# Layer 0 of a four-layer attention stack: queue order, PSUM buffers and row transfers of the attention loop

## The reference, cut to layer 0

```python
h = jnp.concatenate([x, latents], axis=1)
q = (latents @ q_w + q_b).reshape(b, k_len, NH, DH)
kv = (h @ kv_w + kv_b).reshape(b, p + k_len, NH, DH, 2)
kmat, v = (kv[..., 0], kv[..., 1])
attn = jnp.einsum('bkhd,bnhd->bhkn', q, kmat) / DH
attn = jnp.where(full_mask[:, None, None, :], attn, -jnp.inf)
attn = jax.nn.softmax(attn.astype(jnp.float32), axis=-1)
attn_out = jnp.einsum('bhkn,bnhd->bkhd', attn, v).reshape(b, k_len, H)
attn_out = attn_out @ out_w + out_b + residual
out = rmsnorm(attn_out, postnorm_w)
out = jax.nn.gelu(out @ mlp_w1 + mlp_b1) @ mlp_w2 + mlp_b2
return out + residual
```

## Time and profile before

| what | us |
|---|---|
| median of 3 runs | 867.13 (861.98 to 872.77) |
| the profiled execution's own time | 865.07 |
| its span | 863.3 |
| TensorE busy with matmuls | 732.3 (85%) |
| VectorE, ScalarE, GpSimd busy | 502.7, 319.0, 310.6 |
| mean granted TensorE clock | 0.893 |

### The profile page before, as it was taken

One profiled execution on the slowest core, in us unless ns is written; L12 is line 12 of the kernel. 1 busy time (PEld: TensorE's weight loads), 2 busy tenths in 40 slices (PEclk: granted clock), 3 DMA queues, 4 the chain that ended last, 5 costly groups with the idle time before them and its releaser, 6 DMA issues.

```text
span 863.3 us, 11707 instructions
## 1 busy us (share of the span) xinstructions
PE 732.3 (85%) x4432; PEld 526.8 (61%) x4432; DVE 502.7 (58%) x840; ACT 319.0 (37%) x693; POOL 310.6 (36%) x292
## 2 busy tenths in 40 slices
PE   7479885858579687886999999999998999786798
PEld 5356553434259554555776678787566888354587
DVE  6433454554354749986553867433579667388453
ACT  1033322323141137774554222565223241376321
POOL 2020334322202438885330755000467523177200
PEclk7657776787879899999999999999999999987799
DMA  5615444300100050000345000043000000200000
GB/s 171 181 44 152 145 133 119 101 3 1 30 2 1 1 194 1 2 1 2 99 147 179 17 1 0 12 155 128 1 1 0 1 1 1 98 1 0 1 19 32
DMA packets 42073, 46.99 MB, mean 54 GB/s; under 512 B 7009, under 2 KB 36514, under 8 KB 41890
## 3 DMA queue, kind: packets, MB, share of 16 engines
q1 hardware_dynamic: 41456, 45.62, 17.1%
q10 hardware_dynamic: 562, 0.62, 0.3%
HBM read 37.88 MB, written 8.29 MB: 53 GB/s over the span
## 4 chain that ended last, share of the span: by engine, by line
PE 60%; DVE 22%; POOL 5%; issue 4%; DMA 4%; ACT 3%; SPq 2%; ACTq 0%; POOLq 0%; DVEq 0%
PE narrow_ps L459 8%; PE wide_ps L790 7%; PE wide_ps L440 6%; PE narrow_ps L825 5%; PE narrow_ps L638 5%; PE wide_ps L576 4%; PE wide_ps L741 4%; DMA wstream<-in_wqT 3%; PE wide_ps L777 3%; PE wide_ps L490 3%; DVE mx L1407 3%; PE wide_ps L764 2%; DVE scoresb L1334 2%; DVE mx L1343 2%; POOL probs L1633 2%
## 5 line engine op out<-in xcount | busy, mean ns | idle before, releaser
L1624 POOL TENSOR_TENSOR scoresb<-scoresb,mx 128x768 f32<-128x768 f32 (+1 forms) x40 | 70.7, 1767 | 152.9 <-DVE mx L1341 115.1
L1407 DVE TENSOR_REDUCE mx<-wide_ps 128x2 f32<-128x640 f32 x64 | 52.7, 823 | 62.0 <-PE wide_ps L576 62.0
L1633 POOL TENSOR_TENSOR probs<-scoresb,rcp 128x1024 f32<-128x1024 f32 x40 | 77.2, 1929 | 8.0 <-DVE rcp L1351 8.0
L1012 ACT ACTIVATE probsT<-wide_ps 128x1024 f32<-128x1024 f32 x40 | 40.9, 1023 | 105.3 <-PE wide_ps L490 105.3
L459 PE MATMUL narrow_ps<-wstream_r,hidden 128*128 128x256 f32 x576 | 71.9, 285 | 8.0 <-DVE hidden L1319 7.7
L576 PE MATMUL wide_ps<-krow,qrow 49*128 49x64 f32 (+2 forms) x192 | 41.7, 451 | 42.5 <-DVE mx L1407 37.5
L459 PEld LDWEIGHTS narrow_ps<-wstream_r,hidden 128*128 128x128 f32 x576 | 70.9, 192 | 9.5 <-DVE hidden L1319 8.2
L1610 POOL TENSOR_TENSOR rstd<-veps,mhalf 128x1 f32<-128x1 f32 x56 | 32.0, 572 | 121.1 <-DVE veps L1264 121.1
L440 PE MATMUL wide_ps<-xq_r,wstream_r 128*128 128x512 f32 x192 | 64.0, 416 | 9.8 <-issue 5.2
L490 PEld LDWEIGHTS wide_ps<-ident,probs 128*128 128x128 f32 x320 | 39.5, 151 | 48.2 <-issue 47.5
L490 PE MATMUL wide_ps<-ident,probs 128*128 128x128 f32 x320 | 46.3, 292 | 26.5 <-POOL probs L1633 24.7
(11 more groups left out here) (181 smaller groups left out, 1625.7 us busy)
## 6 DMA issues: line engine op xcount, KB each, us to landing
wstream<-in_L_xattn_wk SPq DMA_DIRECT2D x8, 512.0 KB, 4.1
wstream<-in_L_xattn_wv SPq DMA_DIRECT2D x8, 512.0 KB, 5.2
wstream<-in_L_xattn_wo SPq DMA_DIRECT2D x8, 512.0 KB, 6.4
wstream<-in_wqT SPq DMA_DIRECT2D x8, 512.0 KB, 7.9
kscratch<-kparts SPq DMA_DIRECT2D x24, 160.0 KB
krow<-kscratch SPq DMA_DIRECT2D x16, 200.0 KB
qscratch<-qparts SPq DMA_DIRECT2D x24, 128.0 KB
qrow<-qscratch SPq DMA_DIRECT2D x16, 192.0 KB
```

The source lines that it names most:

```text
L1012: nc.scalar.activation(dst, src, ACT.Identity, **kw).then_inc(ring.drained[ring.slot(key)], 1)
L1407: v.tensor_reduce(mx0[:, half % 2, qh, pl:pl + 3:2], ps[:, :, 0:KEYS0], AX, ALU.max).then_inc(wide.drained[wide.slot(key)], 1)
L1624: g.tensor_tensor(s3[:, first:], s3[:, first:], mx[:, u % 3, first:].unsqueeze(2).broadcast_to([P, 16 - first, n_scores]), ALU.subtract).t ...
L1633: g.tensor_tensor(probs[:, u % 2, :].rearrange("p (h k) -> p h k", h=16), s3[:, :, 0:T], rcp[:, u % 3, :].unsqueeze(2).broadcast_to([P, 16 ...
```

## The change

- GpSimd: key sums are issued by `sums_after`: the first three of a group at its last step, the fourth at the next step, each behind that step's rstd. Row additions start at step 9.
- PSUM: maxima alternate between wide buffers 1 and 2; wide buffer 0 is all that is left to the `quarter` ring, two 1-bank buffers. Both of a step's units of maxima follow the scores, "C" follows the maxima (`scores_ctx0`), then the first side job, values, the other jobs. The values' chunks are dealt out as 3, 2, 3.
- Rows: `qscratch` and `kscratch` are laid out head by head. A group's q is stored by 2 DMAs instead of 3, k by 2 instead of 3, k loaded by 3 instead of 4. Context keys come first in `kparts`, the products for them are placed accordingly.
- Start: the constant rows are stored from SP's queue ahead of the values' weights, k of group 0 is stored and loaded from ScalarE's queue after job ("k", 1); SP's order of x, bias and ctxD is new; GpSimd sets slots 1 and 2 of `krow` and `qrow`; ("vctx", 1) moves behind the second half's maxima; the first four units are turned before the other four run.

```diff
-        quarter = Ring([sem(f"quarter{i}_filled") for i in range(4)], [sem(f"quarter{i}_drained") for i in range(4)])
-        quarter_ps = wide_ps[:, 0:2, :].rearrange("p s (h n) -> p (s h) n", h=2)
+        quarter = Ring([sem(f"quarter{i}_filled") for i in range(2)], [sem(f"quarter{i}_drained") for i in range(2)])
+        quarter_ps = wide_ps[:, 0, :].rearrange("p (h n) -> p h n", h=2)
...
-        START0 = [("q", 0), ("k", 0), ("q", 1), ("k", 1), ("v", 0), ("q", 2), ("k", 2), ("vctx", 0), ("vctx", 1)]
+        START0 = [("q", 0), ("k", 0), ("q", 1), ("k", 1), ("v", 0), ("q", 2), ("k", 2), ("vctx", 0)]
-        START_MAX0 = [(half, pl, qh) for half in range(2) for pl in range(2) for qh in range(2)]
-        VALUES0 = {1: (0, 3), 2: (3, 6), 3: (6, 8)}
+        START_MAX0 = [[(half, pl, qh) for pl in range(2) for qh in range(2)] for half in range(2)]
+        VALUES0 = {1: (0, 3), 2: (3, 5), 3: (5, 8)}
+        def sums_after(step):
+            g, p = divmod(step, PAIRS0)
+            if p == 3 and g < GROUPS0:
+                return [step - 3, step - 2, step - 1]
+            return [step - 1] if p == 0 and 0 < g <= GROUPS0 else []
+        def head_rows(scratch, g, first, count):
+            rows_ = scratch[g, :, 0:QK_ROWS].rearrange("h (d s) n -> h d s n", s=3)[:, :, first:first + count]
+            return rows_.rearrange("h d s n -> h d (s n)")
+        def store_q(queue, g):
+            queue.wait_ge(*narrow.empty(("q", g)))
+            queue.dma_start(head_rows(qscratch, g, 0, 1), part_rows(qparts, g, 1)).then_inc(qk_stored[g % 2], 16)
+            queue.dma_start(head_rows(qscratch, g, 1, 2), part_rows(qparts, g, 2)).then_inc(qk_stored[g % 2], 16)
...
+        def wait_slot(queue, g):
+            queue.wait_ge(rows_set[min(g % 3, 1)], 2)
+            if g == 0:
+                queue.wait_ge(const_stored, 80)
...
+            queue.wait_ge(qk_stored[g % 2], 64 * (g // 2 + 1))
+        def load_k(queue, g):
+            wait_slot(queue, g)
+            for i, to, lo, hi in ((0, 2 * T, T, KEYS0), (0, 0, 0, T), (1, T, 0, KEYS0)):
+                queue.dma_start(krow[64 * i:64 * i + QK_ROWS + 2, g % 3, :, to:to + hi - lo].bitcast(F32),
+                                kscratch[g, i::2, :, lo:hi].rearrange("r s n -> s r n")).then_inc(qk_loaded[g % 3], 16)
...
-                ps, filled = take_wide(("M", half, pl, qh), 1, (2,))
+                ps, filled = take_wide(("M", half, pl, qh), 1, (1, 2))
...
-            for unit in START_MAX0:
+            for unit in START_MAX0[0]:
                 max_scores0(*unit)
-            side_product0(("max", 0), (0, 1))
+            side_product0(("max", 0), SIDE)
+            for unit in START_MAX0[1]:
+                max_scores0(*unit)
+            side_product0(("vctx", 1), SIDE)
             for step in range(STEPS0 + 5):
                 g, p = divmod(step, PAIRS0)
                 if step < STEPS0:
                     scores0(step)
-                units = max_units(step)
-                if units:
-                    max_scores0(*units[0])
+                for unit in max_units(step):
+                    max_scores0(*unit)
+                if step < STEPS0:
+                    scores_ctx0(step)
...
             sp.dma_start(*halves(q_w0, t["L0_xattn_q_w"])).then_inc(load["q_w0"], 16)
             sp.dma_start(actT[:, :, 0:S], xT[:, :, 0:S]).then_inc(load["xT0"], 16)
+            v_load(0, "k_w0")
+            sp.wait_ge(maskrow_ready, 1)
+            for b in range(B):
+                sp.dma_start(kscratch[2 * b:2 * b + 2, :, QK_ROWS],
...
+            v_load(1, "v_w0")
...
+            store_q(sp, 0)
+            sp.dma_start(vbias0[:], t["v_b0"].rearrange("(a n) -> a n", a=1).broadcast_to([P, D])).then_inc(load["v_b0"], 16)
+            sp.dma_start(actT[:, :, S:2 * S], xT[:, :, S:2 * S]).then_inc(load["xT1"], 16)
+            store_q(sp, 1)
+            store_k(sp, 1)
+            load_q(sp, 0)
+            sp.dma_start(ctxD[:].rearrange("p c b a k -> p c (b a k)"), t["ctxD"].rearrange("(c p) n -> p c n", p=P)).then_inc(load["ctxD"], 16)
+            load_q(sp, 1)
+            load_k(sp, 1)
+            load_max(0)
...
             for job in START0:
                 side0_copy(job)
+                if job == ("k", 1):
+                    store_k(act, 0)
+                    load_k(act, 0)
...
-            v.memset(krow[:].rearrange("p a r n -> p (a r n)").bitcast(F32), 0.0).then_inc(rows_set, 1)
+            v.memset(krow[:, 0].rearrange("p r n -> p (r n)").bitcast(F32), 0.0).then_inc(rows_set[0], 1)
...
-                if step < STEPS0:
-                    sum_keys0(step)
                 for job, n in side0(step):
                     if job == "proj":
                         rstd_of(0, n)
+                for unit in sums_after(step):
+                    sum_keys0(unit)
```

More of the change, by code:

```diff
@@ L265, in build @@
         link_pool = sem("pool_step")
-        rows_set = sem("rows_set")
+        rows_set = [sem(f"rows_set{i}") for i in range(2)]
         maskrow_ready = sem("maskrow_ready")
@@ L546, in side_product0 @@
                     pe.wait_ge(load["ctxT"], 16)
-                    for off, size, src in ((0, S, actT[:, :, b * S:(b + 1) * S]), (S, T, ctxT[:, :, b * T:(b + 1) * T])):
+                    for off, size, src in ((T, S, actT[:, :, b * S:(b + 1) * S]), (0, T, ctxT[:, :, b * T:(b + 1) * T])):
                         for kc in range(NC):
@@ L580, in take_quarter @@
             def take_quarter(key):
-                s, before = quarter.take(key, 1, (0, 1, 2, 3))
+                s, before = quarter.take(key, 1, (0, 1))
                 if before:
@@ L661, in _ @@
                     values0(g - 1, VALUES0[p])
-                if units:
-                    max_scores0(*units[1])
                 for job in jobs[1:]:
                     side_product0(job, SIDE)
-            for s in range(4):
+            for s in range(2):
                 pe.wait_ge(quarter.drained[s], quarter.owed[s])
@@ L1422, in _ @@
                 side0_copy(job)
-            for unit in START_MAX0:
-                max0(*unit)
+            for half in START_MAX0:
+                for unit in half:
+                    max0(*unit)
+            side0_copy(("vctx", 1))
+            link(v.memset(bvhot[:].rearrange("p a b -> p (a b)"), 0.0))
             for step in range(STEPS0 + 5):
                 g, p = divmod(step, PAIRS0)
-                units = max_units(step)
-                if units:
-                    max0(*units[0])
+                for unit in max_units(step):
+                    max0(*unit)
                 jobs = side0(step)
```

113 lines of the change are left out of this document (48 added, 65 removed).

## The result

The changed kernel takes 813.77 us (median of 4 runs, 813.07 to 816.65) against 867.2 (4 runs, 861.98 to 872.77); the ratio is 0.9389, 95% interval 0.9326 to 0.9452, so it is faster by 6.1%. The profiled execution took 813.47 us, span 811.6; before, 865.07 and 863.3. The forecast was 809 us.

A forecast was written before the change was run, and what follows sets the result against it. TensorE bounds the kernel, through idle waits and a low granted clock. From 865.1 us: 45 off groups 2 to 7, 0 off groups 0 and 1, 6 off the drain, 5 off the start, giving 809; own range 795 to 823, whole 792 to 845.

The forecast's parts named there:

- Rstd ahead of key sums, 22 us: Attention loop and drain: TensorE's stalls of 9.0, about 8 and 5.0 us behind GpSimd's late rstd go, 22 us.
- The bursts: GpSimd's three key sums in a row, 4 us a group, were taken to cost 0.
- Two buffers for maxima: Group ends: TensorE may run two units ahead, leaving 0.5 of the 2.4 us gap; groups 2 to 7 gain 45.
- The floor of 77.3 us: Groups 2 to 7: TensorE's busy time times granted clock, the work at 2.4 GHz without stops.
- 1.8 us a group: Groups 2 to 7: allowance for issue gaps, turn-to-q wait and transfers, 11 us together, giving 88 instead of 133.5.
- Half as many score buffers: Loop: cutting score buffers from four to two costs 0; if uncovered, one exponential, 0.55 us, for each step.
- Groups 0 and 1: Loop's first two groups: busy mostly at low clock, which must rise again; 0 gained, bounds 0 and 6.
- Drain, 17 us: Behind the last group: 23.0 less the 5.0 us stall and 1 for the clock; gain 6, bounds 3 and 8.
- Start, a gain of 5: Before the loop: first maxima at 33 us, scores at 43 instead of 47.81; gain 5, bounds 0 and 12.
- A (824: Rival for the whole: only waits and the start's 5 us go, clock still falls in each group; 824 us, chance 0.22.
- B (843): Rival for the whole: only rstd's stalls go, start gains nothing because ctxD is late; 843 us, chance 0.12.
- C (895): Rival, slower: scores wait for ScalarE with two score buffers, low clock throughout groups 2 to 7; 895 us, chance 0.06.

The follow-up runs named there:

- experiment 1: Kernel before with GpSimd's new order alone and the values' chunks dealt out as 3, 2, 3: 844.59 us, ratio 0.9777.
- experiment 2: Changed kernel with GpSimd's old order (row addition, key sum, then rstd; additions from step 5): 833.45 us, ratio 0.9643.
- experiment 9: Changed kernel with ScalarE's first cast of MLP weights moved from step 16 to 19, VectorE's subtraction from 18 to 20: 804.61 us, ratio 0.9315.
- experiment 6: Kernel before with two of its four score buffers in use, nothing else changed: 875.58 us, ratio 1.0139.
- experiment 7: Changed kernel with the context scores straight behind the step's scores, ahead of the maxima: 819.25 us, ratio 0.9514.
- experiment 4: Changed kernel with the first batches' context values moved from ahead of the first maxima to behind them: 811.73 us, ratio 0.9407.
- experiment 10: Changed kernel with another start: group 0's rows stored and loaded earlier, first values and both context values moved into the loop: 810.32 us, ratio 0.9365.
- experiment 12: Changed kernel with experiment 10's start, experiment 9's later cast and idle transposes ahead of the loop: 800.17 us, ratio 0.9267.
- experiment 8: Changed kernel with DMAs of operand rows not merged, 12 a group again: 809.49 us, ratio 0.938.
- experiment 5: Kernel of experiment 1 with ten idle transposes at the group ends, in groups 2 to 6: 831.39 us, ratio 0.9612.

## Why the prediction was right, point by point

*Rstd ahead of key sums, 22 us.* Right: 19 us alone and 22 on top of the rest, by experiments 1 and 2. VectorE's waits for rstd, 19.5 us in five waits between 48 and 243 us with the 5.11 of the earlier trace rows among them, are down to 2.0 us in three, and GpSimd follows the statistics at once. The bursts cost next to nothing, as taken: the scaling of xn, 344/633/1345 ns in the earlier trace rows, now reads

```profile
L1306 DVE TENSOR_SCALAR xn<-xB,rstd x8: 341/352/646, 110.7 to 190.3; 128x256 f32<-128x256 f32 x8
```

Before, four of the eight took 0.8 us or more, and the three longest of them (1.14, 1.34 and 1.34 us) ran beside key sums; now two are slowed, to 0.62 and 0.65 us, both beside a key sum, one of them within a burst. So not every norm comes a step away from the burst, as the prediction had it, but the price is 0.3 us each. The Trainium skill (SBUF — State Buffer, "Who interferes with whom") explains such a slowdown by a port pair that the two engines share. The traces agree with it: 0.34 us alone, up to 1.34 beside a key sum.

*Two buffers for maxima.* Right in mechanism. The 0.5 us wait of the q product behind the turn is there, 2.4 us in five waits. For groups 2 to 7, 88 us were expected and 93.9 measured, 5.9 us more. The floor of 77.3 us, from busy time times clock, was fair: the rows after give 72.5 by the same working. Above it lie 14.2 us in which TensorE isn't busy and 7.2 us that the low clock of groups 4, 5 and 7 costs. The term that was mis-sized is the one for waits, "1.8 us a group", 11 us together: it had no place for the MLP weights, and none for a clock that falls again. Groups 4 and 5 alone are 18.3 + 18.3, and experiment 9 gives 6 to 9 us back when the cast comes later. The prediction had read every buffer's due time but not that of loads whose reader stands at a fixed step.

*Half as many score buffers, "I take 0".* The argument is right in the part that matters: "the context block waits for the first exponential under the two maxima" names the cover, and experiments 6 and 7 show its worth. Without it halving costs 10.6 to 13 us, and 5 to 11 us are lost again if "C" is moved forward in the changed kernel. The 0 is too low: 7.1 us of waits of the context scores are left, 3.6 of them behind the late weights. The price named for the uncovered case, one exponential at each step's scores, was put at the wrong product: in experiment 6 the context scores wait, 16 times, and not the scores.

*Groups 0 and 1, "0 gained (bounds 0 and 6)".* Wrong: 31.1 instead of 38.8 us, a gain of 7.7, outside the bounds. The step that failed is the sentence that the clock "has to rise from there again". It was already at 0.92 in group 0, whose work is the same (busy time times clock is 7.9 us before and after): the clock rose during the second context values, which now run without a stop into the first scores. In experiment 4, with both context values there, it rose among them too, and group 0 again ran at 1.00 until 58 us. That they are what holds it up isn't shown: experiment 10 (0.55 without them) also has more work in group 0 and a wait of 2.95 us ahead of it, and in experiment 12 the clock was at 1.00 at the first scores and fell all the same.

*Drain, 17 us.* Right: 17.1.

*Start, a gain of 5.* Wrong: 1.9 lost, outside the bounds of 0 and 12. Scores begin at 49.68 us and not at 43. Three steps failed.

The first is a premise. q1 and k1 belong to the first batch and don't need the second batch's x, so they ran at 9.07 to 11.4 us, not until 19.

The second is the sum up to the first maxima. With ctxD issued "at about 24" and the 8.6 us of the earlier trace rows it is there at 32.6, and the context values stand ahead of the maxima and take 3.75 us: 36.4, not 33. The product was left out. Measured: issue at 23.49, 10.2 us to land, first maxima at 37.48. From the turn to the scores it is then 7.4 us instead of 5.7. (Before, ctxD was the queue's seventh issue, not its fifth.)

The third is the memsets, counted as relief for VectorE only. VectorE's conversion of the mask (L1393) must be done before SP stores the constant rows, and all that SP does later stands behind them. It took 1.74 us before. In the changed kernel, and then in experiment 7, it reads

```profile
2.73 3.32 DVE L1393 TENSOR_SCALAR probsT<-probs 1x256 f32<-1x256 int32 x1
4.11 1.80 POOL L1699 MEMSET qrow<- 128x2048 f32 x1
```

```profile
2.74 6.08 DVE L1393 TENSOR_SCALAR probsT<-probs 1x256 f32<-1x256 int32 x1
...
5.86 2.69 POOL L1701 MEMSET vpad<- 128x2048 f32 x2
```

Each time it ends 0.1 to 0.3 us behind the end of a GpSimd memset: 6.05 behind 5.91, 8.82 behind 8.55, and before the change 4.47 behind 4.21. Of the variants all but experiment 4 that start from the changed kernel have the 6.08. Where the start is otherwise as changed (experiments 2, 7, 8 and 9) scores then begin at 51.1 to 52.3 us, against 49.68 and 49.31 with 3.3. No run of the changed kernel leaves these memsets with VectorE, so what they cost isn't shown.

From 24 to 32 us the DMA engines are 95 to 97% busy and ctxD and the rows share them; by experiment 4 both land at about 33.8.

The errors in the sum, +6.9 in the start, -7.7 in groups 0 and 1, +5.9 in groups 2 to 7 and -0.4 behind the loop, leave 4.4 us with the rounding of the sum; 809 was close partly by luck, because two of them cancel. The range has a small slip of its own: starts of 0 to 12 and groups of 80 to 95 us give 794 to 821, not 795 to 823.

Of the signs that the prediction named, most came: rstd follows at once, the maxima's wait is 4.1 us (under 6), the loop takes 142.1 us (under 165), and groups 2 and 6 read 1.00 (14.3 and 12.1 us, where 14 to 16 were named). Two didn't: group 4 has 18.3 us at 0.81, and scores later than 47.8 were the sign for "wrong in the start". Of the rivals, A (824, clock falls in each group) is refuted by the 1.00 of groups 2, 3 and 6, though in groups 4, 5 and 7 it does fall; B (843) was right that the start gains nothing and that ctxD is late, and its number is experiment 1's, not the change's; C (895) had a right worry about two score buffers, at the wrong product.

## What to carry to other kernels

A short stop of TensorE has two prices, its length and the stretch at half clock behind it; multiply busy time by granted clock to see what a stretch would cost without stops, and treat the last stop that remains in a loop as the expensive one. Changes that bring forward a whole loop also bring forward the due times of loads that have nothing to do with it: list the reader of every late load. And when a buffer ring is shortened, look at the tile that is taken out of turn, not at the average rate.

## What the runs showed of the hardware that was not expected

Ten transposes that compute nothing made a kernel 14 us faster (experiment 5). How short a stop makes the clock fall isn't settled: it fell behind the stops of 2.4 us, but also in experiment 5's group 3, where the longest wait was 1.17 us, while groups 2 and 4 held it with the same wait; and in the changed kernel's group 5 behind waits of 0.83 and 0.24 us, while group 6 held it through two waits of the same lengths. Nor did it rise at once where TensorE was hardly ever idle: in experiment 10 it was busy 19.35 of 20.3 us in group 0, nearly all of it at half clock.

While the constant rows of `kscratch` are stored, 160 KB read from a single partition, the DMA engines move a tenth of what they move in the loads just before. Stretches of the changed kernel (us; busy; clock; DMA share; GB/s last):

```profile
4.00:6.00 2.00, 1.77 (x9) 1.50 (x9) 2.00 (x1) 0.00 (x0) 2.00 (x3) 1.00 0.97 336
...
8.00:10.00 2.00, 1.31 (x8) 1.09 (x8) 1.56 (x3) 0.53 (x1) 1.57 (x9) 1.00 0.56 31
10.00:12.00 2.00, 1.45 (x9) 1.18 (x8) 0.48 (x1) 0.98 (x2) 0.67 (x4) 1.00 0.83 26
```

From 10 to 12 us the engines are 83% busy and move 26 GB/s, where loads reach 336. The first stores of group 0's q are issued in the same stretch, and no run tells what makes these transfers slow. The constant rows now stand ahead of group 0's stores; that this delays the start was not tried by itself.
